# Two residual layers, one with a masked weight and one with LoRA: order of the groups and of the start changed

## The chip, the cores and the metric

The kernel runs on one core of one Trainium2 chip. The metric is the device time of one execution in microseconds (us), the median of several.

## The reference

For each of 8 batch elements, x has 256 rows and 1024 columns. D = 1024, the LoRA rank R is 16. In float32:

```
# layer 0: a weight that is changed by a mask, with its own coefficient for each batch element
y = x + x @ W0.T + b0 + coeff[b] * (x @ (2 * mask[b] - 1))
# layer 1: a fixed weight and the LoRA pair of the element's slot
A, B = lora_As[slot[b]], lora_Bs[slot[b]]
z = y + y @ W1.T + b1 + 2.0 * ((y @ A) @ B)
```

## The kernel before, in words

**Precision.** TensorE multiplies operands of the type float32r (fp32r in the rows). Each operand is split into a high part (written by ScalarE as float32r) and a low part (the difference, made by VectorE), and each product is three: high by high, high by low, low by high.

**Layer 0 of a batch element.** The weight of element b is W0 + identity + 2 coeff x mask - coeff. It is made in eight blocks k of 128 x 1024. The mask block is loaded by SP into one of four slots of `ring`. VectorE writes `sums` (weights_sum, L463) over it, ScalarE makes wc_hi from this (weights_high, L338), VectorE makes wc_lo (weights_low, L470), both in rings of four. A mask slot is free again when wc_lo of its block is done. TensorE takes 16 products with wc_hi (layer0_high, L258) and 8 with wc_lo (layer0_low, L267) for each block, summing into four PSUM banks y_ps. Then ScalarE and VectorE write y_two, the parts of y, out of them (y_high L357, y_low L493). x is split the same way (x_high L351, x_low L486).

**Layer 1.** For two halves s of 128 rows, the 16 + 1024 columns of [A, W1] are cut into three groups g, each with its own PSUM bank z_ps. A group is 24 products (layer1_group, L290): eight k by three. Group 0 holds h = y A. h is scaled, split into h_rows (h_high L363, h_low L501), transposed by TensorE (turn_h, L303) and copied to h_stack (h_copy, L368). A closing product of h_stack and b_stack (the parts of B and b1) ends each group (close_group, L311). Then ScalarE copies z_ps to z_rows (z_copy, L375), and stores each half from its own DMA queue (store).

**W1 and LoRA.** W1 is loaded once, through the same ring slots as the masks. GpSimd adds the identity to its diagonal block (L237), ScalarE writes w1_hi (w1_high, L345) and VectorE w1_lo (w1_low, L481). The LoRA pair is loaded for each element (load_lora on SP, one transfer for a_raw and four for b_raw). ScalarE writes the high parts of A and B (lora_high, L386 and L387), and GpSimd both low parts (lora_low, L218 and L221):

```
            def lora_low(b):
                pool.wait_ge(lora_hi_done, 2 * (b + 1))
                pool.tensor_tensor(w1_lo[:, :, 0:R], a_raw[:], w1_hi[:, :, 0:R].bitcast(F32),
                                   ALU.subtract).then_inc(lora_lo_done, 1)
                pool.wait_ge(lora_lo_done, 2 * b + 1)
```

The two low parts of element b bring lora_lo_done to 2b + 1 and 2b + 2. load_lora(b) on SP waits for lora_lo_done >= 2b.

**What sets the order.** Every engine runs an order written out by hand, and semaphores join them. Nothing is planned by a tool. On each engine what stands behind a waiting instruction waits too. Before, TensorE ran layer 0 and layer 1 of one element after the other. At the start SP loads W0, mask and x of element 0 in turns, GpSimd adds the identity to W0's diagonal blocks (L214), makes the parts of b1 (L226 to L231), and then the diagonals of W1. TensorE warms up with 30 transposes (L246).

## Time and profile before

| what | us |
|---|---|
| median of 3 runs | 424.15 (424.01 to 424.44) |
| the profiled execution | 426.43 |
| its span, first to last instruction | 424.6 |
| TensorE products busy | 389.6 (92%) |
| VectorE busy | 228.5 (54%) |
| ScalarE busy | 158.8 (37%) |
| GpSimd busy | 46.1 (11%) |

The span lies inside the profiled execution's time. Busy time of TensorE counts products that overlap in its pipeline, so it is not the share of its peak. PE is TensorE's products, PEld its weight loads, DVE is VectorE, ACT ScalarE, POOL GpSimd, SP the engine that only issues transfers; a q behind a name (SPq, ACTq) is that engine's instruction queue. L12 is line 12 of the kernel.

### The profile page before, as it was taken

Reading aid. Unit: us, or ns where it says so; the run is one execution under the profiler, and the core shown is the slowest. Engines: PE = TensorE matmul, PEld = TensorE weight load, DVE = VectorE, ACT = ScalarE, POOL = GpSimd, SP = SyncE. Lnnn points to the kernel's source line nnn. Section 1 sums busy time; section 2 is a strip of 40 time slices with the busy share of each in tenths; the row PEclk is TensorE's granted clock in tenths of the full one; section 3 lists DMA queues with packets and bytes.
Section 4 is the critical chain, followed back from the end, with each engine's and each line's share of the span. In section 5 each row is a group of like instructions: output and inputs, shape, how many; then the busy total and the mean of one; then the engine's idle time right before and its main releaser. Section 6 shows DMA issues by size and latency. Waiting matters only on the chain.

```text
span 424.6 us, 6715 instructions
## 1 busy us (share of the span) xinstructions
PE 389.6 (92%) x2782; PEld 385.9 (91%) x2782; DVE 228.5 (54%) x265; ACT 158.8 (37%) x282; POOL 46.1 (11%) x43
## 2 busy tenths in 40 slices
PE   5986049999999999999999999999999999999997
PEld 5986049999999999999999999999999999999996
DVE  1788747752584727752474717843475717843300
ACT  2433715341544325341444324341444324432311
POOL 1338340020002000020001100020000100020000
PEclk9799659999999999999999999999999999999999
DMA  8985780665047520665046520675036520520011
GB/s 270 398 271 182 250 277 4 229 220 175 2 145 210 194 78 2 213 234 181 0 137 220 190 82 0 203 243 181 2 129 211 206 82 2 198 100 2 0 51 49
DMA packets 21220, 61.80 MB, mean 146 GB/s; under 512 B 3012, under 2 KB 4292, under 8 KB 21190
## 3 DMA queue, kind: packets, MB, share of 16 engines
q1 hardware_dynamic: 18304, 52.96, 38.2%
q10 hardware_dynamic: 2886, 8.41, 4.9%
q8 instruction: 22, 0.36, 0.3%
q14 instruction: 8, 0.07, 0.0%
HBM read 52.97 MB, written 8.39 MB: 144 GB/s over the span
## 4 chain that ended last, share of the span: by engine, by line
PE 83%; DMA 8%; DVE 3%; issue 2%; ACT 2%; POOL 1%; SPq 1%; ACTq 0%; DVEq 0%
PE z_ps L290 44%; PE y_ps L258 25%; PE y_ps L267 11%; DMA ring<-in_mask 4%; DMA ring<-in_w 2%; PE z_ps L311 2%; DMA w_t<-in_w 2%; ACT y_two L357 1%; DVE wc_lo L470 1%; POOL ring L237 1%; DVE w_lo L481 1%; DVE y_two L493 1%; ACT w_hi L345 1%; PE t_ps L303 0%; DVE ring L463 0%
## 5 line engine op out<-in xcount | busy, mean ns | idle before, releaser
L290 PE MATMUL z_ps<-w_hi,y_two 128*128 128x344 f32 (+1 forms) x768 | 191.5, 325 | 23.2 <-DVE w_lo L481 17.4
L290 PEld LDWEIGHTS z_ps<-w_hi,y_two 128*128 128x128 f32 x768 | 136.4, 190 | 25.2 <-DVE w_lo L481 17.6
L258 PE MATMUL y_ps<-x_two,wc_hi 128*128 128x256 f32 x1024 | 135.1, 285 | 2.7 <-ACT wc_hi L338 2.7
L258 PEld LDWEIGHTS y_ps<-x_two,wc_hi 128*128 128x128 f32 x1024 | 129.5, 194 | 3.0 <-DVE x_two L486 3.0
L290 PE MATMUL z_ps<-w_lo,y_two 128*128 128x344 f32 (+1 forms) x384 | 124.3, 324 | 0.0
L470 DVE SCALAR_TENSOR_TENSOR wc_lo<-ring,coeff_neg,wc_hi 128x1024 fp32r<-128x1024 f32 x64 | 91.5, 1432 | 51.3 <-ACT wc_hi L338 51.0
L338 ACT ACTIVATE wc_hi<-ring,coeff_neg 128x1024 fp32r<-128x1024 f32 x64 | 73.6, 1151 | 69.7 <-PE y_ps L267 41.4
L463 DVE SCALAR_TENSOR_TENSOR ring<-ring,coeff_two,w_t 128x1024 f32<-128x1024 int32 x64 | 82.0, 1290 | 6.5 <-DMA ring<-in_mask 6.4
L267 PE MATMUL y_ps<-x_two,wc_lo 128*128 128x256 f32 x512 | 73.2, 286 | 4.7 <-DVE wc_lo L470 4.7
L290 PEld LDWEIGHTS z_ps<-w_lo,y_two 128*128 128x128 f32 x384 | 73.1, 190 | 0.0
L267 PEld LDWEIGHTS y_ps<-x_two,wc_lo 128*128 128x128 f32 x512 | 66.7, 194 | 5.8 <-DVE wc_lo L470 5.8
L493 DVE SCALAR_TENSOR_TENSOR y_two<-y_ps,b_cols,y_two 128x256 fp32r<-128x256 f32 x64 | 25.8, 476 | 64.7 <-ACT y_two L357 64.7
L357 ACT ACTIVATE y_two<-y_ps,b_cols 128x256 fp32r<-128x256 f32 x64 | 24.1, 486 | 67.1 <-PE y_ps L267 67.1
L218 POOL TENSOR_TENSOR w_lo<-a_raw,w_hi 128x128 fp32r<-128x128 f32 x8 | 3.7, 457 | 300.5 <-ACT b_stack L387 300.5
L375 ACT ACTIVATE z_rows<-z_ps 128x344 f32<-128x344 f32 (+1 forms) x48 | 20.0, 451 | 38.2 <-PE z_ps L311 38.2
L501 DVE SCALAR_TENSOR_TENSOR h_rows<-z_ps,h_rows 128x16 fp32r<-128x16 f32 x32 | 4.1, 170 | 45.7 <-ACT h_rows L363 45.7
L486 DVE TENSOR_TENSOR x_two<-x_raw,x_two 128x512 fp32r<-128x512 f32 x32 | 21.1, 696 | 12.3 <-ACT x_two L351 12.3
L363 ACT ACTIVATE h_rows<-z_ps 128x16 fp32r<-128x16 f32 x32 | 4.1, 181 | 54.6 <-PE z_ps L290 54.6
L351 ACT ACTIVATE x_two<-x_raw 128x512 fp32r<-128x512 f32 x32 | 18.5, 626 | 5.7 <-DMA x_raw<-in_x 5.7
L221 POOL TENSOR_TENSOR b_stack<-b_raw,b_stack 32x1024 fp32r<-32x1024 f32 x8 | 19.0, 2380 | 0.6
L481 DVE TENSOR_TENSOR w_lo<-ring,w_hi 128x1024 fp32r<-128x1024 f32 x8 | 11.2, 1436 | 4.5 <-ACT w_hi L345 4.5
L311 PE MATMUL z_ps<-b_stack,h_stack 66*128 66x344 f32 (+1 forms) x48 | 12.7, 318 | 0.0
(25 smaller groups left out, 74.0 us busy)
## 6 DMA issues: line engine op xcount, KB each, us to landing
ring<-in_mask SPq DMA_DIRECT2D x64, 512.0 KB, 3.6
x_raw<-in_x SPq DMA_DIRECT2D x32, 256.0 KB, 5.8
out<-z_rows ACTq DMA_DIRECT2D x14, 512.0 KB, 5.0
w_t<-in_w SPq DMA_DIRECT2D x8, 512.0 KB, 7.3
ring<-in_w SPq DMA_DIRECT2D x8, 512.0 KB, 4.3
b_raw<-in_lora_b SPq DMA_DIRECT2D x32, 64.0 KB, 2.6
out<-z_rows ACTq DMA_DIRECT2D x2, 340.0 KB, 2.2
a_raw<-in_lora_a SPq DMA_DIRECT2D x8, 64.0 KB, 2.8
```

Of the source, the lines that this page charges most:

```text
L221: pool.tensor_tensor(b_stack[2 * R:LR, :], b_raw[2 * R:LR, :], b_stack[2 * R:LR, :].bitcast(F32), ALU.subtract).then_inc(lora_lo_done, 1)
L258: pe.matmul(ys, w, x_two[:, k, n, :], start=(k == 0 and o % PAIR == 0 and n == 0), stop=False, skip_group_check=True)
L267: ins = pe.matmul(ys, w, x_two[:, k, 0, :], start=False, stop=(k == KT - 1), skip_group_check=True)
L290: ins = pe.matmul(z_ps[g][:, 0:EDGES[g + 1] - EDGES[g]], ys[:, k, s * P:(s + 1) * P], w[:, k, EDGES[g]:EDGES[g + 1]], start=(k == 0 and n ...
L311: pe.matmul(z_ps[g][:, lo:EDGES[g + 1] - EDGES[g]], h_stack[0:KS, s * P:(s + 1) * P], b_stack[0:KS, EDGES[g] + lo - R:EDGES[g + 1] - R], s ...
L338: act.activation(wc_hi[:, k % RING, :], sums[:, mask_entry(b, k) % RING, :], ACT.Identity, bias=coeff_neg[:, b:b + 1]).then_inc(wc_hi_done, 1)
L357: act.activation(y_two[:, b % 2, 0, o, :], y_ps[g][:, (o % PAIR) * T:(o % PAIR + 1) * T], ACT.Identity, bias=b0_cols[:, o:o + 1]).then_inc ...
L375: act.activation(z_rows[:, s, EDGES[g] + lo - R:EDGES[g + 1] - R], z_ps[g][:, lo:EDGES[g + 1] - EDGES[g]], ACT.Copy).then_inc(z_done, 1)
L463: dve.scalar_tensor_tensor(out=sums[:, e % RING, :], in0=ring[:, e % RING, :], scalar=coeff_two[:, b:b + 1], in1=w0_t[:, k, :], op0=ALU.mu ...
L470: dve.scalar_tensor_tensor(out=wc_lo[:, k % RING, :], in0=sums[:, mask_entry(b, k) % RING, :], scalar=coeff_neg[:, b:b + 1], in1=wc_hi[:, ...
L486: dve.tensor_tensor(x_two[:, PAIR * g:PAIR * (g + 1), 1, :], x_raw[:, PAIR * g:PAIR * (g + 1), :], x_two[:, PAIR * g:PAIR * (g + 1), 0, :] ...
L493: dve.scalar_tensor_tensor(out=y_two[:, b % 2, 1, o, :], in0=y_ps[g][:, (o % PAIR) * T:(o % PAIR + 1) * T], scalar=b0_cols[:, o:o + 1], in ...
```

## The change

It has three parts.

1. The last group of layer 1 (s = 1, g = 2) with its closing product moves behind layer 0 of the next element (layer1_last). ScalarE and VectorE run y_high, y_low, x_high and x_low at the head of their turn, and z_copy and store of that last group come behind them. lora_high is split: the A half stands behind z_copy(a, 1, 1), the B half behind the moved z_copy and store.
2. Element 0 is worked in half blocks of 512 columns, each with a wait of its own (parts). Layer 1 of element 0 opens with layer1_first, which goes through W1 block by block for all three groups of s = 0. Group (0, 1, 0) uses the bank y_ps[3].
3. W0's blocks 1 to 7 are loaded from ScalarE's queue, the first block in halves from SP's, and the first x through ScalarE's queue. SP loads the LoRA pair of element 0 behind the fourth W1 block.

lora_low on GpSimd is as before. The diff, cut to its core:

```diff
+        def parts(b, k, h=1):
+            return 2 * k + h + 1 if b == 0 else KT * (b + 1) + k + 1
...
+        def z_bank(b, s, g):
+            return y_ps[XG - 1] if (b, s, g) == (0, 1, 0) else z_ps[g]
...
+            sp.dma_start(w0_t[:, 0, 0:HALF], w0[0, :, 0:HALF]).then_inc(w0_first, 16)
+            sp.dma_start(ring[:, 0, 0:HALF], mask_v[0, 0][:, 0:HALF]).then_inc(mask_first, 16)
+            sp.dma_start(w0_t[:, 0, HALF:D], w0[0, :, HALF:D]).then_inc(w0_in[0], 16)
+            sp.dma_start(ring[:, 0, HALF:D], mask_v[0, 0][:, HALF:D]).then_inc(ring_in[0], 16)
+            for k in range(1, KT):
                 load_mask(0, k)
-                if k % PAIR == 0:
-                    load_x(0, k // PAIR)
+                if k % PAIR == 1 and k < KT - 1:
+                    load_x(0, k // PAIR + 1)
+            for k in range(RING):
+                load_w1(k)
             sp.wait_ge(ids_in, 16)
             load_lora(0)
-            for k in range(KT):
+            for k in range(RING, KT):
...
             def layer0_high(b, k):
                 pe.wait_ge(x_lo_done, XG * b + k // PAIR + 1)
-                pe.wait_ge(wc_hi_done, KT * b + k + 1)
+                if b > 0:
+                    pe.wait_ge(wc_hi_done, parts(b, k))
                 for o in range(KT):
+                    if b == 0 and o % HT == 0:
+                        pe.wait_ge(wc_hi_done, parts(b, k, o // HT))
                     if k == 0 and o % PAIR == 0:
                         need(pe, y_lo_done, KT * (b - 1) + o + PAIR)
+                    if b == 1 and k == 0 and o == KT - PAIR:
+                        pe.wait_ge(z_done, NG + 1)
...
+            def products(b, s, g, k):
+                y_hi, y_lo = y_two[:, b % 2, 0], y_two[:, b % 2, 1]
+                for n, (ys, w) in enumerate(((y_hi, w1_hi), (y_hi, w1_lo), (y_lo, w1_hi))):
+                    ins = pe.matmul(z_bank(b, s, g)[:, 0:EDGES[g + 1] - EDGES[g]], ys[:, k, s * P:(s + 1) * P],
+                                    w[:, k, EDGES[g]:EDGES[g + 1]],
+                                    start=(k == 0 and n == 0), stop=(g == 0 and k == KT - 1 and n == 2),
+                                    skip_group_check=True)
+                if g == 0 and k == KT - 1:
+                    ins.then_inc(h_full, 1)
+            def layer1_first():
+                pe.wait_ge(lora_lo_done, 1)
+                for k in range(KT):
+                    pe.wait_ge(w1_lo_done, k + 1)
+                    pe.wait_ge(y_lo_done, k + 1)
+                    for g in range(NG):
+                        products(0, 0, g, k)
             def layer1_group(b, s, g, ks=range(KT)):
                 if ks[0] == 0:
-                    need(pe, z_done, NG * (ST * b + s - 1) + g + 1)
-                    if b == 0 and s == 0 and g == 0:
-                        pe.wait_ge(w1_lo_done, KT)
+                    if (b, s, g) != (0, 1, 0):
+                        need(pe, z_done, NG * (ST * b + s - 1) + g + 1)
                     if s == 0 and g == 0:
-                        pe.wait_ge(lora_lo_done, 2 * (b + 1))
-                y_hi, y_lo = y_two[:, b % 2, 0], y_two[:, b % 2, 1]
+                        pe.wait_ge(lora_lo_done, 2 * b + 1)
                 for k in ks:
                     if s == 0 and g == 0:
                         pe.wait_ge(y_lo_done, KT * b + k + 1)
-                    for n, (ys, w) in enumerate(((y_hi, w1_hi), (y_hi, w1_lo), (y_lo, w1_hi))):
-                        ins = pe.matmul(z_ps[g][:, 0:EDGES[g + 1] - EDGES[g]], ys[:, k, s * P:(s + 1) * P],
-                                        w[:, k, EDGES[g]:EDGES[g + 1]],
-                                        start=(k == 0 and n == 0), stop=(g == 0 and k == KT - 1 and n == 2),
-                                        skip_group_check=True)
-                if g == 0 and ks[-1] == KT - 1:
-                    ins.then_inc(h_full, 1)
+                    products(b, s, g, k)
...
                     pe.wait_ge(h_stacked, ST * b + s + 1)
-                pe.matmul(z_ps[g][:, lo:EDGES[g + 1] - EDGES[g]], h_stack[0:KS, s * P:(s + 1) * P],
+                    pe.wait_ge(lora_lo_done, 2 * (b + 1))
+                pe.matmul(z_bank(b, s, g)[:, lo:EDGES[g + 1] - EDGES[g]], h_stack[0:KS, s * P:(s + 1) * P],
...
             def layer1(b):
                 for s in range(ST):
-                    layer1_group(b, s, 0)
-                    layer1_group(b, s, 1, range(KT // 2))
-                    turn_h(b, s)
-                    layer1_group(b, s, 1, range(KT // 2, KT))
-                    close_group(b, s, 0)
-                    close_group(b, s, 1)
-                    layer1_group(b, s, 2)
-                    close_group(b, s, 2)
+                    if b > 0:
+                        layer1_group(b, s, 0)
+                        layer1_group(b, s, 1, range(HT))
+                        turn_h(b, s)
+                        layer1_group(b, s, 1, range(HT, KT))
+                        close_group(b, s, 0)
+                        close_group(b, s, 1)
+                    elif s == 0:
+                        layer1_first()
+                        layer1_group(0, 1, 0, range(HT))
+                        turn_h(0, 0)
+                        layer1_group(0, 1, 0, range(HT, KT))
+                        close_group(0, 0, 0)
+                        close_group(0, 0, 1)
+                    if s == 0 and b > 0:
+                        layer1_group(b, 0, 2)
+                    if s == 0:
+                        close_group(b, 0, 2)
+                    if s == 1 and b == 0:
+                        layer1_group(0, 1, 1, range(HT))
+                        turn_h(0, 1)
+                        layer1_group(0, 1, 1, range(HT, KT))
+                        close_group(0, 1, 0)
+                        close_group(0, 1, 1)
+            def layer1_last(b):
+                layer1_group(b, 1, 2)
+                close_group(b, 1, 2)
             pe.wait_ge(ident_done, 1)
             warm_up(30)
-            for b in range(NB):
+            layer0(0)
+            layer1(0)
+            for b in range(1, NB):
                 layer0(b)
+                layer1_last(b - 1)
                 layer1(b)
+            layer1_last(NB - 1)
...
-            def lora_high(b):
+            def lora_a_high(b):
                 act.wait_ge(lora_in, 16 * 5 * (b + 1))
+                if b > 0:
+                    act.wait_ge(z_full, NG * (ST * b - 1) + 1)
+                act.activation(w1_hi[:, :, 0:R], a_raw[:], ACT.Copy).then_inc(lora_hi_done, 1)
+            def lora_b_high(b):
                 need(act, z_full, NG * ST * b)
-                act.activation(w1_hi[:, :, 0:R], a_raw[:], ACT.Copy).then_inc(lora_hi_done, 1)
                 act.activation(b_stack[0:LR, :], b_raw[0:LR, :], ACT.Copy).then_inc(lora_hi_done, 1)
...
+            for k in range(1, KT):
+                act.dma_start(w0_t[:, k, :], w0[k]).then_inc(w0_in[k], 16)
...
-            for k in range(RING):
-                w1_high(k)
-            lora_high(0)
+            w1_high(0)
+            w1_high(1)
+            lora_a_high(0)
             act.wait_ge(b0_in, 16)
             for g in range(XG):
                 y_high(0, g)
-            for k in range(RING, KT):
+            for k in range(2, KT):
                 w1_high(k)
-            for b in range(1, NB):
+            lora_b_high(0)
+            for b in range(1, NB + 1):
                 a = b - 1
+                if a > 0:
+                    for g in range(XG):
+                        y_high(a, g)
+                if b < NB:
+                    for g in range(XG):
+                        x_high(b, g)
+                if a > 0:
+                    z_copy(a - 1, 1, 2)
+                    store(a - 1, 1)
+                    lora_b_high(a)
                 h_high(a, 0)
-                x_high(b, 0)
-                x_high(b, 1)
                 h_copy(a, 0)
-                x_high(b, 2)
-                x_high(b, 3)
-                weights_high(b, 0)
+                if b < NB:
+                    weights_high(b, 0)
                 z_copy(a, 0, 0)
                 z_copy(a, 0, 1)
-                weights_high(b, 1)
+                if b < NB:
+                    weights_high(b, 1)
+                    weights_high(b, 2)
                 z_copy(a, 0, 2)
                 store(a, 0)
                 h_high(a, 1)
-                weights_high(b, 2)
+                if b < NB:
+                    weights_high(b, 3)
                 h_copy(a, 1)
-                weights_high(b, 3)
                 z_copy(a, 1, 0)
                 z_copy(a, 1, 1)
-                z_copy(a, 1, 2)
-                store(a, 1)
-                lora_high(b)
-                for k in range(RING, KT):
-                    weights_high(b, k)
-                for g in range(XG):
-                    y_high(b, g)
-            a = NB - 1
+                if b < NB:
+                    lora_a_high(b)
+                    for k in range(RING, KT):
+                        weights_high(b, k)
+            store(NB - 1, 1, 0, 2)
+            z_copy(NB - 1, 1, 2)
+            store(NB - 1, 1, 2, 3)
...
-            x_low(0, 0)
-            for k in range(KT - 1):
-                step(0, k)
-                if k % PAIR == 0 and k < KT - PAIR:
-                    x_low(0, k // PAIR + 1)
-            weights_low(0, KT - 1)
-            for k in range(RING):
-                w1_low(k)
+            for k in range(KT):
+                weights_sum(0, k, 0)
+                if k % PAIR == 0:
+                    x_low(0, k // PAIR)
+                weights_sum(0, k, 1)
+                weights_low(0, k, 0)
+                weights_low(0, k, 1)
+            w1_low(0)
+            w1_low(1)
             dve.wait_ge(b0_in, 16)
             for g in range(XG):
                 y_low(0, g)
-            for k in range(RING, KT):
+            for k in range(2, KT):
                 w1_low(k)
             for b in range(1, NB):
                 a = b - 1
+                if a > 0:
+                    for g in range(XG):
+                        y_low(a, g)
+                for g in range(XG):
+                    x_low(b, g)
                 h_low(a, 0)
-                x_low(b, 0)
-                x_low(b, 1)
-                x_low(b, 2)
-                x_low(b, 3)
                 weights_sum(b, 0)
                 step(b, 0)
                 step(b, 1)
+                step(b, 2)
                 h_low(a, 1)
-                for k in range(2, KT):
+                for k in range(3, KT):
                     step(b, k)
-                for g in range(XG):
-                    y_low(b, g)
+            for g in range(XG):
+                y_low(NB - 1, g)
```

## Rows read from the trace of the kernel before

**Rows 1.** The page, its first line.

```profile
span 424.6 us, 6715 instructions
...
```

**Rows 2.** Chain of waits: start us, us, what (x instructions merged).

```profile
...
59.13 8.09 PE z_ps L290 x36
...
85.45 1.91 PE y_ps L258 x16
...
105.60 1.92 PE y_ps L258 x16
...
109.30 5.96 PE z_ps L290 x36
...
121.49 5.75 PE z_ps L290 x36
...
129.55 3.77 PE z_ps L290 x24
133.48 1.91 PE y_ps L258 x16
...
```

**Rows 3.** Waits: engine line <- releaser: total us, times, longest us.

```profile
...
PE z_ps L290 <- DVE y_two L493: 5.8, 7, 0.8
...
PE y_ps L267 <- DVE wc_lo L470: 4.7, 4, 2.2
...
```

**Rows 4.** Timeline of ScalarE, 104 to 137 us: start, us, operation.

```profile
...
107.79 3.02 ACT L357 ACTIVATE y_two<-y_ps,b_cols 128x256 fp32r<-128x256 f32 x8 [9.59 <-PE y_ps L267]
...
113.55 1.15 ACT L351 ACTIVATE x_two<-x_raw 128x512 fp32r<-128x512 f32 x2
...
133.52 0.46 ACT L375 ACTIVATE z_rows<-z_ps 128x344 f32<-128x344 f32 x1 [3.29 <-PE z_ps L311]
...
134.45 0.31 ACT L386 ACTIVATE w_hi<-a_raw 128x128 fp32r<-128x128 f32 x1 [0.47 <-ACT z_rows L375]
134.66 1.04 ACT L387 ACTIVATE b_stack<-b_raw 64x1024 fp32r<-64x1024 f32 x1
...
```

**Rows 5.** Timeline of GpSimd, 104 to 137 us.

```profile
...
135.79 0.46 POOL L218 TENSOR_TENSOR w_lo<-a_raw,w_hi 128x128 fp32r<-128x128 f32 x1 [45.07 <-ACT b_stack L387]
...
```

**Rows 6.** Timeline of VectorE, 104 to 137 us.

```profile
...
108.67 3.23 DVE L493 SCALAR_TENSOR_TENSOR y_two<-y_ps,b_cols,y_two 128x256 fp32r<-128x256 f32 x8 [9.14 <-ACT y_two L357]
...
116.23 1.29 DVE L486 TENSOR_TENSOR x_two<-x_raw,x_two 128x512 fp32r<-128x512 f32 x2 [0.72 <-ACT x_two L351]
...
```

**Rows 7.** Timeline of all engines, 0 to 90 us.

```profile
...
12.23 1.28 DVE L470 SCALAR_TENSOR_TENSOR wc_lo<-ring,coeff_neg,wc_hi 128x1024 fp32r<-128x1024 f32 x1
...
24.81 0.33 SPq L158 DMA_DIRECT2D ring<-in_mask  x1
...
26.59 1.89 SPq L178 DMA_DIRECT2D b_raw<-in_lora_b  x4
...
34.19 5.37 DVE L470 SCALAR_TENSOR_TENSOR wc_lo<-ring,coeff_neg,wc_hi 128x1024 fp32r<-128x1024 f32 x2
...
52.57 2.59 POOL L237 TENSOR_TENSOR ring<-ring,ident 128x128 f32<-128x128 f32 x1 [2.52 <-DMA ring<-in_w]
...
```

**Rows 8.** The page, transfers: KB each, median us from issue to landing.

```profile
...
ring<-in_w SPq DMA_DIRECT2D x8, 512.0 KB, 4.3
b_raw<-in_lora_b SPq DMA_DIRECT2D x32, 64.0 KB, 2.6
...
```

**Rows 9.** Windows: us, busy by engine, granted clock (PEclk), DMA share, GB/s.

```profile
...
7.10:9.10 2.00, 0.00 (x0) 0.00 (x0) 0.45 (x1) 1.11 (x2) 0.00 (x0) 1.00 1.00 401
9.30:15.80 6.50, 5.98 (x26) 5.72 (x27) 3.38 (x5) 2.14 (x3) 2.10 (x3) 0.50 1.03 413
16.00:46.60 30.60, 21.02 (x167) 20.00 (x165) 25.32 (x19) 12.41 (x14) 16.09 (x13) 1.00 0.76 252
46.80:63.60 16.80, 4.47 (x15) 4.48 (x16) 10.07 (x13) 7.37 (x13) 6.25 (x5) 0.50 0.81 277
63.80:424.60 360.80, 352.18 (x2546) 350.01 (x2544) 187.36 (x228) 133.84 (x250) 19.90 (x14) 1.00 0.37 123
...
```

More of the change, by code:

```diff
@@ L30, in cond_residual_two_layers @@
     KS = LR + 2
+    HALF = D // 2
+    HT = KT // 2
     assert PAIR == 2 and ST == 2 and XG == 4 and LR == 64 and KT == 2 * RING and NB > 2
@@ L211, in _ @@
             for k in range(KT):
-                pool.wait_ge(w0_in[k], 16)
+                pool.wait_ge(w0_first if k == 0 else w0_in[k], 16)
                 blk = w0_t[:, k, k * P:(k + 1) * P]
@@ L335, in weights_high @@
             def weights_high(b, k):
-                act.wait_ge(sum_done, KT * b + k + 1)
                 block_read(act, b, k - RING)
-                act.activation(wc_hi[:, k % RING, :], sums[:, mask_entry(b, k) % RING, :], ACT.Identity,
-                               bias=coeff_neg[:, b:b + 1]).then_inc(wc_hi_done, 1)
+                e = mask_entry(b, k)
+                for lo, hi in ((0, HALF), (HALF, D)) if b == 0 else ((0, D),):
+                    act.wait_ge(sum_done, parts(b, k, lo // HALF) if b == 0 else parts(b, k))
+                    act.activation(wc_hi[:, k % RING, lo:hi], sums[:, e % RING, lo:hi], ACT.Identity,
+                                   bias=coeff_neg[:, b:b + 1]).then_inc(wc_hi_done, 1)
             def w1_high(k):
@@ L375, in z_copy @@
                 act.activation(z_rows[:, s, EDGES[g] + lo - R:EDGES[g + 1] - R],
-                               z_ps[g][:, lo:EDGES[g + 1] - EDGES[g]], ACT.Copy).then_inc(z_done, 1)
+                               z_bank(b, s, g)[:, lo:EDGES[g + 1] - EDGES[g]], ACT.Copy).then_inc(z_done, 1)
             def store(b, s, g0=0, g1=NG):
@@ L442, in _ @@
-            a = NB - 1
-            for s in range(ST):
-                h_high(a, s)
-                h_copy(a, s)
-                z_copy(a, s, 0)
-                z_copy(a, s, 1)
-                store(a, s, 0, 2)
-                z_copy(a, s, 2)
-                store(a, s, 2, 3)
-            for s in range(ST):
-                act.wait_ge(z_out[s], 16 * (NB + 1))
+                if b < NB:
+                    lora_a_high(b)
+                    for k in range(RING, KT):
+                        weights_high(b, k)
@@ L456, in _, with weights_sum @@
+            store(NB - 1, 1, 0, 2)
+            z_copy(NB - 1, 1, 2)
+            store(NB - 1, 1, 2, 3)
+            for s in range(ST):
+                act.wait_ge(z_out[s], 16 * (NB + s))
         @block.vector
         def _(dve):
-            def weights_sum(b, k):
+            def weights_sum(b, k, h=None):
                 e = mask_entry(b, k)
-                ring_filled(dve, e)
-                if b == 0:
+                lo, hi = (0, D) if h is None else (HALF * h, HALF * (h + 1))
+                if (b, k, h) == (0, 0, 0):
+                    dve.wait_ge(mask_first, 16)
+                else:
+                    ring_filled(dve, e)
+                if b == 0 and k // HT == h:
@@ L462, in weights_sum @@
                     dve.wait_ge(w0_diag, k + 1)
-                dve.scalar_tensor_tensor(out=sums[:, e % RING, :], in0=ring[:, e % RING, :],
-                                         scalar=coeff_two[:, b:b + 1], in1=w0_t[:, k, :],
+                elif b == 0:
+                    dve.wait_ge(w0_in[k], 16)
+                dve.scalar_tensor_tensor(out=sums[:, e % RING, lo:hi], in0=ring[:, e % RING, lo:hi],
+                                         scalar=coeff_two[:, b:b + 1], in1=w0_t[:, k, lo:hi],
@@ L465, in weights_sum, with weights_low @@
                                          op0=ALU.mult, op1=ALU.add).then_inc(sum_done, 1)
-            def weights_low(b, k):
-                dve.wait_ge(wc_hi_done, KT * b + k + 1)
-                dve.wait_ge(sum_done, KT * b + k + 1)
-                dve.scalar_tensor_tensor(out=wc_lo[:, k % RING, :], in0=sums[:, mask_entry(b, k) % RING, :],
-                                         scalar=coeff_neg[:, b:b + 1], in1=wc_hi[:, k % RING, :].bitcast(F32),
+            def weights_low(b, k, h=None):
+                lo, hi = (0, D) if h is None else (HALF * h, HALF * (h + 1))
+                n = parts(b, k) if h is None else parts(b, k, h)
+                dve.wait_ge(wc_hi_done, n)
+                dve.wait_ge(sum_done, n)
+                dve.scalar_tensor_tensor(out=wc_lo[:, k % RING, lo:hi], in0=sums[:, mask_entry(b, k) % RING, lo:hi],
+                                         scalar=coeff_neg[:, b:b + 1], in1=wc_hi[:, k % RING, lo:hi].bitcast(F32),
```

21 lines of the change are left out of this document (11 added, 10 removed).

## The prediction

> **What bounds the kernel now.** I read the page first: TensorE is busy for most of the 424.6 us span [rows 1]. The chain of waits then shows where it is not. From 85.45 us on it repeats every 48.03 us (85.45 to 133.48) [rows 2]: layer 0 ends at 105.60 + 1.92 + 0.96 = 108.48, layer 1 begins at 109.30, and the next layer 0 at 133.48. The list of waits puts seven waits of 0.8 us on the residual y_two (L493) [rows 3]. So the steady part holds 0.82 us of idle TensorE in each batch, and a first stretch of 36 products that takes 5.96 instead of 5.75 us, as it follows y_two block by block: 1.03 us a batch, 7.2 us in all. That is all that the steady part has to give. The other reserve is the start: layer 1 of batch 0 begins only at 59.13 [rows 2].
>
> **The steady part: what is removed, and what comes in its place.** Behind layer 0 of batch b now stand the 24 products and the closing product of batch b-1's last group: 133.48 - 129.55 = 3.93 us [rows 2]. In that time ScalarE and VectorE can make y_two, so the 1.03 us go. But look at what layer 1 of b waits for besides y_two. layer1_group(b, 0, 0) waits for lora_lo_done >= 2b + 1, the low part of the A columns, which GpSimd makes in lora_low (L216). That function is not in the diff, and its first line waits for lora_hi_done >= 2(b + 1), both high copies. The change splits these: A's is early, but B's (lora_b_high) now stands on ScalarE behind y_high(a), x_high(b) and z_copy(a-1, 1, 2) of the same turn. So A's low part, which needs nothing of B, comes after B's copy. Before, both copies were made early in layer 0 (134.45 and 134.66 [rows 4]) and nobody waited.
>
> I walk that queue on the clock of batch 1, where layer 0 ends at 108.48. The eight y_high run from 107.79 for 3.02 us, to 110.81. Four x_high follow, 1.15 us for each two [rows 4]: 2.30, to 113.11. The moved group is over at 108.48 + 3.93 = 112.41, so z_copy can start at 113.11. From z_copy's start to that of B's copy it is 134.66 - 133.52 = 1.14 us, store's issue included, less 0.21 for A's copy, which is no longer between them: 0.93 [rows 4]. From B's copy to GpSimd's subtraction it is 135.79 - 134.66 = 1.13, the subtraction takes 0.46 [rows 5], and waking TensorE 0.14 (the first y_low ends 0.49 after 108.67, TensorE starts at 109.30 [rows 2, 6]). Sum 2.66: layer 1 starts at 115.77, TensorE has been idle for 3.36 us. VectorE's four x_low end near 114.5 (108.67 + 3.23 + 4 x 0.65 [rows 6]), so GpSimd meets nobody. In the last batch there is no x_high, z_copy starts right at 112.45, and the idle time is 2.70. Together 6 x 3.36 + 2.70 = 22.9 us.
>
> Other queues: load_lora(b) on SP now waits until that subtraction, with masks 4 to 7 of b behind it. Their ring slots are freed by wc_lo(b, 0) some 9 us into layer 1, later than that; cost nothing, and if the cover were gone, layer 0 would start late by as much. The sums of batch b start after h_low(a, 0), sooner in layer 1 than now; layer 0 has four blocks ready. The wait for z_done = 4 before y_ps[3] (once, batch 1) has 12 products in front of it, 1.4 us, against two z copies: nothing.
>
> From layer 0 of batch 1 to the end: 424.6 - 85.45 = 339.15 before; plus 3.93 for batch 0's group, which was before that point; less 7.2; plus 22.9: 358.8 us.
>
> **Layer 1 of batch 0.** Before it took 85.45 - 59.13 = 26.32 us, some 2.3 of it by the half clock [rows 2]. Without the moved group 22.4. Two waits are new. Group (0, 1, 1) needs z_ps[1], free only after two copies: 0.6 us. And the transpose of h(0, 1) waits for h_low(0, 1), which on VectorE stands behind step(1, 2). With T for the moment when h(0, 0) is full: sums 0 and 1 until T + 3.1, wc_lo 0 waits for wc_hi 0 (behind h_copy) and ends at T + 5.9, wc_lo 1 waits for wc_hi 1 (behind two z copies) and ends at T + 8.4, sum 3 and wc_lo 2 until T + 10.9, h_low until T + 11.1. TensorE reaches the transpose at T + 7.9. It waits 3.2 us. Sum 22.4 + 3.8 = 26.2.
>
> **The start.** "Layer 1 follows W1" does not happen, for the reason above: layer1_first waits for lora_lo_done >= 1, so for lora_b_high(0), which ScalarE makes after w1_high(7), and GpSimd after its eight w1 diagonals. All of W1 is there when it starts. When is that? Halves save one half of sum, copy and difference on the first block, 1.6 us: wc_lo 0 ends at 11.9 instead of 12.23 + 1.28 = 13.5 [rows 7]; TensorE's first product stays about where it is, as ScalarE now issues eight more transfers before its first copy. Then VectorE is the bound: four half operations of 0.65 [rows 6] and 0.15 of waiting for ScalarE make 2.75 a block, 7 x 2.75 + 3 x 0.65 for x_low = 21.2, to 33.1. GpSimd's b1 chain falls into this: beside it two full operations took 5.37 us instead of 2.5 and ended at 39.56 [rows 7]. I add 3.5 for it and 0.9 for the diagonals: wc_lo 7 ends at 37.5 (36 to 39).
> From there, in us behind it: SP issues the fourth W1 block, and only then the lora transfers; 1.78 from the block's issue to the first of b_raw, 1.4 to the last [rows 7]; landing 2.6 by its median, 3.1 taken [rows 8]: 6.4. lora_a_high waits for that and has y_high behind it: 6.8. y_high and y_low 108.67 + 3.23 - 107.79 = 4.1 [rows 4, 6]: 10.9. w1_low 2 and 3, 1.2 each: 13.3; W1's last block is issued then and lands 4.3 later [rows 8]: 17.7. Diagonal 0.5, or 2.59 beside VectorE [rows 7], 1.5 taken; w1_high, as wide as B's copy, 1.05; B's copy 1.14; subtraction and waking 0.7: 22.1. So layer 1 starts at 37.5 + 22.1 = 59.6 (57.5 to 62), against 59.13: what the halves give, the late lora load takes back. W0 on ScalarE's queue changes no sum: from 9.30 to 15.80 the engines of both queues were full, share 1.03 at 413 GB/s [rows 9]. The Trainium skill (Trainium Kernel Development and Optimization, Key Constraints) says that several issuing engines save issue time only; by it the term is the same nothing, and the trace agrees as far as it goes, one queue filled the engines.
>
> Sum without the clock: 59.6 + 26.2 + 358.8 = 444.6 us, 20.0 above the span.
>
> **The clock.** Eight idle times of 2.7 to 3.4 us are new in a stream that ran at full clock. The granted clock was 1.00 in the idle time from 7.10 to 9.10, and 0.50 (1.2 GHz) from 9.30 to 15.80; it was 1.00 (2.4 GHz) from 16.00 to 46.60, with a wait of 2.2 us in it [rows 3, 9]. So an idle time near 2 us has been answered in both ways, and these are longer. I take six falls of eight. Price of one: TensorE worked from 59.13 to 63.80 at half clock, 4.67 us, half of it lost: 2.3 (8.09 for 36 products instead of 5.75 says the same [rows 2]). The lower bound is nothing, the upper 5.98 / 2 = 3.0 [rows 9]. 6 x 2.3 = 13.8.
>
> Span 444.6 + 13.8 = 458.4, +33.8. The profiled execution took 426.43 with 424.6 of span; the median is 424.15. Forecast 424.15 + 33.8 = 458.0.
>
> **Rivals.** (A) The forecast: the queue behind B's copy stalls layer 1 in each batch, and the clock falls at four to eight of the stalls: 451 to 468. Chance 0.68. (B) The same stalls, but the clock mostly holds (none to three falls): 442 to 451. For it speaks the 2.2 us wait without a fall, against it 7.10 to 9.30. Chance 0.28. The Trainium skill (TensorE: Matmul & The Clock Gate, What's actually happening) says that the ramp penalty is under 1% of a typical kernel; by that rule the clock would add at most some 4 us, so about 448, in B. Its section on HAM oscillation describes the contrary, a pause in each turn that makes each turn start cold. (C) The other side: the chain to A's low part fits under the moved group, and the time is 424.15 + 0.5 - 0.1 + 3.9 - 7.2 = 421, or 416 if layer 1 of batch 0 starts 5 us sooner as well. It decides where the eight waits sum to less than 2.9 us, 0.4 for each of the seven batches and nothing in batch 0. The walk gives 3.36, with 2.66 of it behind z_copy, which can't start before 112.41. Chance 0.03, with no change 0.01.
>
> The measurement of this kernel tells about 0.2% from no change. Faster 0.03, same 0.01, slower 0.96. The low end of the range, 443, is B with one early start; the high end, 466, is A with eight falls and 62 for the start cut at one in ten.
>
> **What would show it.** Waits: TensorE L290's successor waits on GpSimd's L218 successor, seven times near 3.3 us (the last 2.7), and no longer on y_two. The period is 50.4 us plus the clock. The granted clock is below 1.00 behind several stalls. GpSimd's A subtraction follows B's copy at once. At the start TensorE's layer 1 begins at 57.5 to 62, in one block of 72 products without waits for W1. wc_lo 7 ends at 36 to 39. One wait of 3.2 us for h_low in batch 0. I am wrong if GpSimd's subtraction comes before layer 0 ends, or if the waits are there and something else has shrunk.

## The result, and the profile after

| | us |
|---|---|
| median after (4 runs) | 457.77 (457.31 to 458.28) |
| median before beside it (4 runs) | 424.29 (424.01 to 425.89) |
| ratio after to before | 1.078 (95% interval 1.075 to 1.081) |
| forecast | 458.0, range 443 to 466 |
| span after, granted clock over it | 456.5, 0.94 |

The change makes the kernel 7.8% slower. The waits of TensorE after the change, out of the list of waits (engine, line, what it waited for, total us, times, longest):

```profile
PE z_ps L304 <- issue: 20.1, 7, 2.9
PE z_ps L304 <- POOL w_lo L232: 18.3, 1, 18.3
...
PE t_ps L338 <- issue: 2.8, 1, 2.8
...
PE z_ps L304 <- ACT z_rows L439: 0.6, 1, 0.6
```

The seven waits of 0.8 us for y_two [rows 3] are gone, and seven waits of up to 2.9 us, 20.1 in all, stand in their place. The list calls their end "issue": it found no releaser for them. The queues of the other engines tell who it is. Here are ScalarE and GpSimd in the turn that answers to [rows 4, 5] (timelines, start and us):

```profile
109.47 3.03 ACT L421 ACTIVATE y_two<-y_ps,b_cols 128x256 fp32r<-128x256 f32 x8 [9.65 <-PE y_ps L290]
112.33 2.23 ACT L415 ACTIVATE x_two<-x_raw 128x512 fp32r<-128x512 f32 x4
114.41 0.50 ACT L439 ACTIVATE z_rows<-z_ps 128x344 f32<-128x344 f32 x1
...
115.34 1.06 ACT L456 ACTIVATE b_stack<-b_raw 64x1024 fp32r<-64x1024 f32 x1 [0.43 <-ACT z_rows L439]
```

```profile
116.47 0.45 POOL L232 TENSOR_TENSOR w_lo<-a_raw,w_hi 128x128 fp32r<-128x128 f32 x1 [53.09 <-ACT b_stack L456]
117.00 2.35 POOL L235 TENSOR_TENSOR b_stack<-b_raw,b_stack 32x1024 fp32r<-32x1024 f32 x1
```

GpSimd had been idle for 53.09 us, waiting for B's high part. It ends A's low part at 116.92, and TensorE starts at 117.02. The moved group was over at 113.77 + 0.32 = 114.09 (timeline of TensorE):

```profile
113.77 0.32 PE L347 MATMUL z_ps<-b_stack,h_stack 66*128 66x344 f32 x1
117.02 0.56 PE L304 MATMUL z_ps<-w_hi,y_two 128*128 128x352 f32 x1 [2.93 <-issue]
```

And the clock (windows of TensorE: us, busy, granted clock, DMA share, GB/s), in the wait and in the 5.1 us behind it:

```profile
114.02:117.02 3.00, 0.07 (x1) 1.00 0.41 171
117.02:118.72 1.70, 1.70 (x6) 0.52 0.06 17
118.72:120.42 1.70, 1.70 (x8) 0.50 0.00 0
120.42:122.12 1.70, 1.70 (x12) 0.97 0.38 121
```

It is 1.00 through the wait, and 0.52 and 0.50 (1.2 GHz) once work is back, from 117.02 to 120.42. The chain of waits gives the price of each fall by the first 36 products behind a wait; these are three turns, the first of them also with its undisturbed second half (5.76, against 5.75 in [rows 2]):

```profile
87.11 1.92 PE y_ps L278 x16
...
117.02 7.52 PE z_ps L304 x36
...
130.78 5.76 PE z_ps L304 x36
...
138.84 1.92 PE y_ps L278 x16
...
168.75 7.34 PE z_ps L304 x36
...
220.28 8.71 PE z_ps L304 x36
```

The seven took 7.52, 7.34, 8.71, 7.50, 7.52, 7.48 and 7.40 us: 13.2 us over 7 x 5.76. The first turn is 138.84 - 87.11 = 51.73 us long, against 48.03; less its 1.76 us of slow products it is 49.97, where the forecast had 50.4.

The start: 72 products without a wait for W1 between them, from 60.59, and layer 0 of batch 1 at 87.11 (59.13 and 85.45 before, [rows 2]).

```profile
60.59 14.06 PE z_ps L304 x72
```

### The profile page after: what moved, and what is told of

It is laid out like the page before. It is cut to its first block, busy times and chain, and to the rows that moved or that the text cites. A ratio compares the mean times of both kernels' runs of the same rounds, so it can differ in the third digit from the quotient of the medians.

```text
span 456.5 us, 6779 instructions
## 1 busy us (share of the span) xinstructions
PE 402.7 (88%) x2782; PEld 397.4 (87%) x2782; DVE 225.9 (49%) x281; ACT 161.4 (35%) x290; POOL 39.1 (9%) x43
## 4 chain that ended last, share of the span: by engine, by line
PE 74%; ACT 10%; issue 7%; DVE 4%; DMA 2%; ACTq 2%; SPq 1%; POOL 0%; DVEq 0%
PE z_ps L304 37%; PE y_ps L278 24%; PE y_ps L290 11%; ACT y_two L421 4%; ACT x_two L415 3%; DVE ring L542 2%; ACT wc_hi L402 2%; PE z_ps L347 1%; DMA ring<-in_w 1%; ACTq L465 1%; PE y_ps L304 1%; ACT z_rows L439 1%; DVE wc_lo L551 1%; DVE y_two L574 1%; DMA b_raw<-in_lora_b 1%
## 5 line engine op out<-in xcount | busy, mean ns | idle before, releaser
L304 PE MATMUL z_ps<-w_hi,y_two 128*128 128x344 f32 (+1 forms) x752 | 197.1, 339 | 39.0 <-issue 20.1
L304 PEld LDWEIGHTS z_ps<-w_hi,y_two 128*128 128x128 f32 x752 | 141.9, 202 | 41.8 <-issue 21.9
L278 PE MATMUL y_ps<-x_two,wc_hi 128*128 128x256 f32 x1024 | 136.8, 287 | 6.0 <-DVE x_two L567 4.2
L304 PE MATMUL z_ps<-w_lo,y_two 128*128 128x344 f32 (+1 forms) x376 | 126.9, 338 | 0.0
L551 DVE SCALAR_TENSOR_TENSOR wc_lo<-ring,coeff_neg,wc_hi 128x1024 fp32r<-128x1024 f32 (+1 forms) x72 | 86.8, 1210 | 49.9 <-ACT wc_hi L402 48.5
L402 ACT ACTIVATE wc_hi<-ring,coeff_neg 128x1024 fp32r<-128x1024 f32 (+1 forms) x72 | 75.8, 1056 | 67.6 <-PE y_ps L290 50.5
L542 DVE SCALAR_TENSOR_TENSOR ring<-ring,coeff_two,w_t 128x1024 f32<-128x1024 int32 (+1 forms) x72 | 84.6, 1187 | 6.4 <-DMA ring<-in_mask 6.4
L304 PEld LDWEIGHTS z_ps<-w_lo,y_two 128*128 128x128 f32 x376 | 76.1, 202 | 0.0
L439 ACT ACTIVATE z_rows<-z_ps 128x344 f32<-128x344 f32 (+1 forms) x47 | 20.0, 459 | 33.8 <-PE z_ps L347 33.8
L567 DVE TENSOR_TENSOR x_two<-x_raw,x_two 128x512 fp32r<-128x512 f32 x32 | 22.3, 752 | 2.1 <-ACT x_two L415 2.1
L432 ACT ACTIVATE h_stack<-t_ps 66x128 fp32r<-66x128 f32 x16 | 4.4, 273 | 21.2 <-PE t_ps L338 21.2
```

Of the source, the lines that this page charges most:

```text
L278: pe.matmul(ys, w, x_two[:, k, n, :], start=(k == 0 and o % PAIR == 0 and n == 0), stop=False, skip_group_check=True)
L304: ins = pe.matmul(z_bank(b, s, g)[:, 0:EDGES[g + 1] - EDGES[g]], ys[:, k, s * P:(s + 1) * P], w[:, k, EDGES[g]:EDGES[g + 1]], start=(k == ...
L402: act.activation(wc_hi[:, k % RING, lo:hi], sums[:, e % RING, lo:hi], ACT.Identity, bias=coeff_neg[:, b:b + 1]).then_inc(wc_hi_done, 1)
L439: act.activation(z_rows[:, s, EDGES[g] + lo - R:EDGES[g + 1] - R], z_bank(b, s, g)[:, lo:EDGES[g + 1] - EDGES[g]], ACT.Copy).then_inc(z_do ...
L542: dve.scalar_tensor_tensor(out=sums[:, e % RING, lo:hi], in0=ring[:, e % RING, lo:hi], scalar=coeff_two[:, b:b + 1], in1=w0_t[:, k, lo:hi] ...
L551: dve.scalar_tensor_tensor(out=wc_lo[:, k % RING, lo:hi], in0=sums[:, mask_entry(b, k) % RING, lo:hi], scalar=coeff_neg[:, b:b + 1], in1=w ...
```

## The experiments

Kernel n is the kernel of experiment n; where nothing else is said, its edit is made to the changed kernel. The edits are shortened, and x_high(b, 0..3) stands for four calls. Each kernel was timed beside the kernel before on the same chip. Before measured 425.1 to 425.3 us there, 0.8 to 1.0 more than beside the changed kernel, so differences against the changed kernel are uncertain by 1 us.

**1. A's low part waits for A's high part alone, from batch 1 on.**

```diff
 def lora_low(b):
-    pool.wait_ge(lora_hi_done, 2 * (b + 1))
+    pool.wait_ge(lora_hi_done, 2 * b + 1 if b > 0 else 2)
     pool.tensor_tensor(w1_lo[:, :, 0:R], a_raw[:], w1_hi ...)
+    pool.wait_ge(lora_hi_done, 2 * (b + 1))
     pool.wait_ge(lora_lo_done, 2 * b + 1)
```

> The changed kernel with one thing more: from element 1 on, GpSimd's low part of the A columns waits for ScalarE's high part of A alone, and only the low part of B waits for B's. My theory (layer 1 waits for A's low part, which is late only because it stands behind B's high part, and the clock falls in that wait): the seven waits of 20.1 us in all go, and the 13.2 us of half clock behind them go with them, so 457.8 - 33.3 = 424.5 us, granted clock 1.00 from batch 1 on. Rival one (the place of the wait is taken by the next in the queue, y_two or h behind the four x_high): a wait of 1 to 2 us stays in each batch and some of the falls, 435 to 445 us. Rival two (the slower first products have another cause than the wait, for instance VectorE reading the same banks): the waits go, the slow products stay, 437.7 us.

Measured 426.26 us, ratio 1.002 (1.000 to 1.004). The span fell from 456.5 to 423.8. The seven waits and their slow products are gone; layer 1 follows the moved group without a gap (chain of waits, where line 305 is the changed kernel's 304):

```profile
110.77 3.79 PE z_ps L305 x24
...
114.72 5.75 PE z_ps L305 x36
```

One line of waiting cost 31.5 us. The time is 1.8 us above the expected 424.5. The kernel before stood 1.0 us higher beside this kernel than beside the changed one, and the 2.8 us wait in batch 0 brought a fall of the clock here, which it did not in the changed kernel's profile: the 12 products behind it took 2.94 instead of 1.88 us (chain of waits):

```profile
84.01 2.94 PE z_ps L305 x12
```

What is left is a change that gains in the steady part and loses as much at the start; kernel 4 tells the two apart.

**2. The wait is filled with products.**

```diff
 layer1_last(b - 1)
+for _ in range(17):
+    pe.matmul(t_ps[:, 0:344], y_two[:, (b - 1) % 2, 0, 0, P:2 * P], w1_hi[:, 0, EDGES[2]:EDGES[3]], start=True, stop=True)
 layer1(b)
```

> The changed kernel, with 17 more products of 344 columns on TensorE between the moved group and layer 1 of each batch from 1 on; they write a bank that nobody reads then (0.157 us each, 2.67 us of the 2.9 us wait), so no term of the output changes. Layer 1 still waits for A's low part as long as before. My theory of the clock (it falls because TensorE is idle, and the slow first products are nothing else): the waits stay at 2.9 us, filled, the clock stays 1.00, and the 13.2 us go: 457.8 - 13.2 = 444.6 us. Rival (the first products are slow for another reason): no change, 457.8 us. Rival (17 products are too many): up to 2 us more.

Measured 446.82, ratio 1.051 (1.048 to 1.054). The clock stays at 1.00 and the first 36 products take 6.00 us (chain of waits):

```profile
115.11 2.65 PE t_ps L386 x17
...
118.06 6.00 PE z_ps L304 x36
```

So 11 of the 33.5 us are the clock alone: the wait is as long, only not idle. The time is 2.2 us above the expected. The seven first stretches took 5.96 to 6.00 and not 5.76 us, 1.5 us in all; and the 2.8 us wait in batch 0 brought a fall as in kernel 1, with the same 2.94 us for the 12 products behind it.

**3. The same early low part for batch 0 too**, behind the fourth W1 diagonal.

```diff
     pool.tensor_tensor(blk, blk, ident[:], ALU.add).then_inc(w1_diag, 1)
+    if k == RING - 1:
+        lora_a_low(0)
+lora_b_low(0)
-for b in range(NB):
-    lora_low(b)
+for b in range(1, NB):
+    lora_a_low(b)
+    lora_b_low(b)
```

> As the first of these kernels, but for batch 0 too: GpSimd makes the low part of A's columns of batch 0 behind the fourth diagonal of W1, so layer 1 of batch 0 can really go through W1 block by block. My theory: its first products start near 47 us instead of 60.6, and by the time that the last W1 block is split (60.2 us) only its own nine products are left, so h(0, 0) is full near 61.7 instead of 73.7. Then h_low(0, 0) stands behind four x_low until 65, and layer 0 of batch 1 starts some 14 us behind that, near 79 to 80 instead of 87.1: 424.5 - 7.5 = 417 us. Rival (TensorE's products are so slow at half clock, 2.8 us a block, that they stay behind W1): 420 to 422. Rival (W1 arrives later, as GpSimd waits for the LoRA load between two diagonals): 420 to 424.

Measured 416.01, ratio 0.979 (0.976 to 0.982). Now layer 1 does follow W1 (timeline of TensorE): its first product is at 47.20, and the last W1 block lets it wait once.

```profile
47.20 0.63 PE L311 MATMUL z_ps<-w_hi,y_two 128*128 128x352 f32 x1 [5.54 <-DVE y_two L581]
...
60.57 0.43 PE L311 MATMUL z_ps<-w_hi,y_two 128*128 128x352 f32 x1 [1.26 <-DVE w_lo L569]
```

**4. The steady part alone**, on the start of before, with the early low part. The orders of ScalarE and VectorE in the turn are those of the change.

```diff
 # kernel before, and:
 for b in range(1, NB):
     layer0(b)
+    layer1_last(b - 1)
     layer1(b)      # without its last group
```

> The kernel before with only the first part of the change, the last group of layer 1 behind the next layer 0, and A's low part waiting for A's high part alone; the start is that of before. My theory: seven waits for y_two of 0.8 us and the 0.2 us in the first products behind each go, and nothing else: 424.3 - 7.2 = 417.1 us. Rival (the order of the queues in the turn, x_high and x_low ahead of h, costs TensorE waits elsewhere in the batch): 418 to 424. If this comes out at 417 and the first of these kernels at 424.5, the start as changed costs about 7 us by itself.

Measured 418.97, ratio 0.985 (0.983 to 0.988), 6.3 us under its own before. That is 1.9 us above the expected 417.1 and in the range of the rival, but the rival's cause is not there: from layer 0 of batch 1 (81.14) to the end the list of TensorE's waits is empty, and a turn takes 128.18 - 81.14 = 47.04 us, 1.0 less than before, as expected. 1.0 us of the miss is the kernel before, which measured that much more beside this kernel than beside the changed one; the rest stays open. Against kernel 1, whose turn is as long, it is the start alone: 426.26 - 418.97 = 7.3 us. The start of the change, as long as nothing follows W1, is a loss: a start of layer 1 that comes later (58.16 here, 60.50 in kernel 1) and the two waits in batch 0.

**5. The LoRA pair of batch 0 ahead of W1**, on kernel 3.

```diff
-for k in range(RING):
-    load_w1(k)
 sp.wait_ge(ids_in, 16)
 load_lora(0)
-for k in range(RING, KT):
+for k in range(KT):
     load_w1(k)
```

> The third kernel (A's low part early in all batches) with one thing undone: SP loads the LoRA pair of batch 0 before the first four W1 blocks, as in the kernel before, instead of behind them. My theory (the late LoRA load holds ScalarE before y_high for 4.6 to 5 us, and y_low, w1_low 2 and 3 and W1's last two blocks follow in its train): the last W1 block is split near 56.5 instead of 60.5, and the time is 416.0 - 3.6 = 412.4 us. Rival (W1's last block is late because of its own ring slots and not of that load): 416.

Measured 412.31, ratio 0.968 (0.965 to 0.971), 3.7 us under kernel 3. y_low starts at 42.47 instead of 46.57 and the last w1_low at 55.46 instead of 59.29 (timeline of VectorE, kernel 5):

```profile
42.47 3.21 DVE L581 SCALAR_TENSOR_TENSOR y_two<-y_ps,b_cols,y_two 128x256 fp32r<-128x256 f32 x8
...
55.46 1.23 DVE L569 TENSOR_TENSOR w_lo<-ring,w_hi 128x1024 fp32r<-128x1024 f32 x1 [1.50 <-ACT w_hi L416]
```

**6. Whole blocks in batch 0**: the start of before, but layer1_first and kernel 3's early low part.

```diff
-for lo, hi in ((0, HALF), (HALF, D)) if b == 0 else ((0, D),):
+for lo, hi in ((0, D),):
...
-w1_low(0)
-w1_low(1)
+for k in range(RING):
+    w1_low(k)
 dve.wait_ge(b0_in, 16)
```

> The start of the kernel before (whole blocks, W0 on SP's queue, LoRA before W1, w1_low 0 to 3 before y_low), but layer 1 of batch 0 goes through W1 block by block, and A's low part is early; the steady part is the changed one. My theory (half blocks bring nothing, as wc_lo 7 ended at 39.81 with them and at 39.56 without): the same as the kernel with the LoRA load first, 412.4 us, within 1.5. Rival (the halves do bring something that the LoRA load hides): 414.5 to 416.

Measured 411.92, ratio 0.968 (0.966 to 0.971), the time of kernel 5. But two things differ from kernel 5: the halves are gone, and W0 is back on SP's queue, which is worth 1.9 us in kernel 8. So the equal times do not show that the halves bring nothing. wc_lo 7 ended at 35.18 + 3.45 = 38.63 here, at 39.76 in kernel 5 (halves, W0 on ScalarE's queue), and at 37.46 in kernel 8 (halves, W0 on SP's).

**7. h first**, on kernel 6, in batch 1's turn. ScalarE's order follows: h_high(0, 1) stands behind the first two z copies.

```diff
 # VectorE, a == 0
+h_low(0, 0)
 x_low(1, 0..3)
-h_low(0, 0)
 weights_sum(1, 0)
+h_low(0, 1)
 step(1, 0); step(1, 1); step(1, 2)
-h_low(0, 1)
```

> The whole-block start that follows W1, and in batch 1's turn VectorE takes h_low(0, 0) before the four x_low and h_low(0, 1) behind the first sum, and ScalarE h_high(0, 1) behind the two first z copies. My theory (in batch 0 TensorE waits 3.3 us for the transpose of h(0, 0) and 1.3 for that of h(0, 1) only because these stand behind other work): about 4 us less than the same kernel without it, 408.4 us. Rival (the sums of batch 1 come later and layer 0 of batch 1 waits for them instead): 411 to 412.5.

Measured 408.37, ratio 0.961 (0.958 to 0.964), 3.55 us under kernel 6. Kernel 6 had one wait of 2.8 us for a transpose of h in TensorE's list of waits; kernel 7 has none.

**8. W0 on SP's queue**, on kernel 3.

```diff
 # SP
 for k in range(1, KT):
+    sp.dma_start(w0_t[:, k, :], w0[k])
     load_mask(0, k)
 # ScalarE
-for k in range(1, KT):
-    act.dma_start(w0_t[:, k, :], w0[k])
```

> The third kernel with W0's blocks 1 to 7 on SP's queue again, each before its mask block; x of the first group stays on ScalarE's queue. The forecast said that moving W0 changes no sum. My theory: ScalarE loads its table 4.4 us sooner, but x lands no sooner, so the first block gains about 1 us, and VectorE's own work sets the rest: 415.0 to 416.0 us against 416.0. Rival (W0 in turns with the masks lets both arrive late, masks 6 and 7 above all): 417 to 420.

Measured 414.06, ratio 0.974 (0.970 to 0.977): 1.9 us less than kernel 3. The two were timed at different times, so this is a small difference. The traces bear it out: VectorE takes up the second half of the first block at 8.41 here and at 10.32 in kernel 3, and wc_lo 7 ends at 35.91 + 1.55 = 37.46 instead of 38.01 + 1.42 = 39.43. Both expectations are missed, on the side of more gain. The changed kernel's ScalarE (its timeline) shows why: seven issues of 0.6 us, then the table, and only then its first copy, at 9.24. In kernel 8 the first copy starts at 7.14.

```profile
3.24 4.44 ACTq L465 DMA_DIRECT2D w_t<-in_w  x7
7.71 1.28 ACT L467 ACT_TABLE_LOAD   x1 [7.71 <-issue]
...
9.24 0.63 ACT L415 ACTIVATE x_two<-x_raw 128x512 fp32r<-128x512 f32 x1
```

**9. b1's parts behind the sixth W1 diagonal**, on kernel 7.

```diff
-pool.wait_ge(b1_in, 32)
-pool.tensor_copy(b_stack[LR:KS, :], b_raw[LR:KS, :])
-pool.tensor_tensor(b_stack[LR:KS, :], b_raw[LR:KS, :], b_stack[LR:KS, :], ALU.subtract)
-pool.tensor_copy(b_stack[LR:LR + 1, :], b_raw[LR:LR + 1, :])
...
     if k == RING - 1:
         lora_a_low(0)
+    if k == RING + 1:
+        pool.wait_ge(w1_diag, k + 1)
+        pool.wait_ge(b1_in, 32)
+        pool.tensor_copy(b_stack[LR:KS, :], b_raw[LR:KS, :])
+        pool.tensor_tensor(b_stack[LR:KS, :], b_raw[LR:KS, :], b_stack[LR:KS, :], ALU.subtract)
+        pool.tensor_copy(b_stack[LR:LR + 1, :], b_raw[LR:LR + 1, :])
```

> The whole-block kernel with h first, and GpSimd makes the three parts of b1 behind W1's sixth diagonal instead of between W0's last and W1's first. My theory (these three instructions hold up VectorE's sums and differences of blocks 6 and 7 of batch 0 by some 3.5 us, and everything up to layer 1 of batch 0 follows in their train): 408.4 - 3.0 = 405.4 us. Rival (the chain now holds up w1_low or the last W1 diagonals as much): 408 to 409.

Measured 404.38, ratio 0.952 (0.949 to 0.955), the fastest of all. wc_lo 7 ends at 31.35 + 2.68 = 34.03 us; in kernel 7 it ended at 34.54 + 3.45 = 37.99, 4.0 us later, as much as the time differs.

**10. x_high behind B's high part**, on the changed kernel.

```diff
-x_high(b, 0..3)
 z_copy(a - 1, 1, 2)
 store(a - 1, 1)
 lora_b_high(a)
+x_high(b, 0..3)
```

> The changed kernel with the four x_high of each turn behind lora_b_high instead of ahead of z_copy; A's low part still waits for B's high part. The forecast's walk says that the chain can't start before z_full of the moved group, whatever stands before it, and takes 2.66 us from there. So the wait falls from 2.9 to 2.6 us in six batches, the clock still falls: 457.8 - 2 = 455.8 us. Rival (the length of ScalarE's queue is what makes the wait, so 2.1 us less in each): 440 to 445.

Measured 455.67, ratio 1.072 (1.068 to 1.076). The waits are 18.2 us in all, 2.6 the longest: ScalarE's queue is shorter by four copies and only 0.3 us a turn comes of it. z_copy's place behind the moved group sets the wait.

```profile
PE z_ps L304 <- issue: 18.2, 7, 2.6
```

**11. The moved group alone, as in the change**: kernel 4 with lora_low as it was.

```diff
-pool.wait_ge(lora_hi_done, 2 * b + 1)
+pool.wait_ge(lora_hi_done, 2 * (b + 1))
...
-pool.wait_ge(lora_hi_done, 2 * (b + 1))
```

> The kernel before with the first part of the change alone, exactly as in the change: the last group behind the next layer 0, lora_high split, lora_low as it was. The start is that of before. My theory (the whole loss is in this part, and the other two parts cost some 7 us more): the 419.0 us of the same kernel with an early low part of A, plus 20.1 us of waits and 13.2 us of half clock: 452 us. Rival (the loss needs the new start too): below 440.

Measured 452.81, ratio 1.066 (1.063 to 1.069). That is 33.8 us over kernel 4. The seven waits are 20.2 us, as in the changed kernel:

```profile
PE z_ps L290 <- issue: 20.2, 7, 3.0
```

**12. All of it with half blocks.**

```diff
+def lora_a_low(b):
+    pool.wait_ge(lora_hi_done, 2 * b + 1)
...
+    sp.dma_start(w0_t[:, k, :], w0[k])
...
+load_lora(0)
 for k in range(RING):
     load_w1(k)
...
+h_low(0, 0)
...
+    if k == RING + 1:
+        pool.wait_ge(w1_diag, k + 1)
```

It is the changed kernel with the edits of 3, 5, 7, 8 and 9.

> The changed kernel's half blocks with all that was found put together: A's low part early, W0 on SP's queue, LoRA before W1, h first in batch 1's turn, b1 behind W1's sixth diagonal. If the terms add up (412.3 for the kernel with the LoRA load first, less 2.0 for W0, less 3.6 for h, less 3.0 for b1): 403.7 us, and the halves are worth about 1.7 us against the same with whole blocks. Rival (they cover each other, as the end of the W1 stream binds): 405 to 408.

Measured 405.67, ratio 0.955 (0.951 to 0.958). The terms don't add up, the rival holds: wc_lo 7 ends at 34.37, 0.3 us after that of kernel 9 (34.03), and the last two w1_low start at 52.02 against 51.30. This start is 1.3 us slower than that of kernel 9 instead of 1.7 faster. It has more in it than the halves, though: w1_high and w1_low of W1's blocks 2 and 3 stand behind y_high and y_low here and ahead of them in kernel 9, and y_low starts at 37.56 against 41.85. VectorE waited 2.62 us for w1_high ahead of the last two w1_low, 1.51 in kernel 9. Which of the two costs the time no run tells apart, so what half blocks are worth by themselves stays open.

## Why the prediction was right

| term | forecast | measured |
|---|---|---|
| layer 1 of batch 0 starts | 59.6 (57.5 to 62) | 60.59 |
| from there to layer 0 of batch 1 | 26.2 | 26.52 |
| seven waits | 22.9 | 20.1 |
| the clock | 13.8 | 13.2 |
| span | 458.4 | 456.5 |

That the median came out 0.2 us from the forecast is partly luck. The span was 1.9 us too high. The forecast put the growth of the span on before's median, but before's profiled execution, from which the growth is reckoned, was 2.3 us above that median (426.43 against 424.15), and the changed kernel's only 0.5 above its own (458.28 against 457.77). The two errors nearly cancel.

**The main step** held: lora_low's first wait ties A's low part to B's high part, and that stands behind z_copy of the moved group. Kernel 1 changes this wait alone and takes 31.5 us off; kernel 11 has it without the new start and pays 33.8 us against kernel 4. Kernel 10 confirms the floor: the chain can't start before the moved group ends, and the forecast's 2.66 us from there was 2.6.

**The wait** was 2.93 us and not 3.36. Nearly all of the difference lies in "four x_high follow, 1.15 us for each two": ScalarE started the first at 112.33, ahead of y_high's end, and z_copy at 114.41, 2.08 later instead of 2.30. In the last turn, without x_high, it was 2.60 for 2.70. The 0.93 and 1.13 us of the chain behind were met to the hundredth (115.34 - 114.41, 116.47 - 115.34).

**The clock.** Forecast were six falls at 2.3 us. There were seven, one at each wait in front of layer 1, at 1.6 to 3.0 us, 1.9 on average; the eighth wait, 2.8 us in batch 0, was followed by none in this profile, and by one in kernels 1, 2 and 10, with the same 2.82 us. Number and price were off in opposite directions, so that 13.2 for 13.8 is in part luck as well. Rival (B), none to three falls, is out, and so is a price under 1% of the span: 13.2 of 456.5 us are 2.9%. Kernel 2 shows that idleness brings the falls: with the same wait filled, none of the seven is left. The Trainium skill (TensorE: Matmul & The Clock Gate, HAM oscillation) describes a pause in each turn that makes each turn start cold; here a pause of 2.9 us in a turn of 51.7 does it.

**The start** came out 1.0 us late, as the sum of two errors. wc_lo 7 ended at 39.81, past the stated 36 to 39. One term that failed is "four half operations of 0.65": that is the length of x_low, and sums and differences of half blocks took 0.70 to 0.82 us. Three half sums took 0.95, each beside a diagonal of GpSimd (at 17.01, 23.97 and 32.93). So a block took 3.0 to 3.3 us, 3.7 with x_low, and not 2.75 and 3.4. The b1 chain was rightly sized, 3.5 forecast and some 3.3 measured. The other is the first block, which ended at 12.8 and not 11.9: ScalarE's seven issues of W0 took 4.44 us, its first copy started at 9.24 instead of 7.99, and "TensorE's first product stays about where it is" was wrong too (10.65 against 9.80).

```profile
38.39 1.42 DVE L551 SCALAR_TENSOR_TENSOR wc_lo<-ring,coeff_neg,wc_hi 128x512 fp32r<-128x512 f32 x2 [0.19 <-ACT wc_hi L402]
```

Against that the train behind wc_lo 7 was shorter, 20.8 us for 22.1. And "W0 on ScalarE's queue changes no sum" was wrong: kernel 8 puts about 2 us on it. It was argued from the DMA engines, which were full either way, and put nothing for ScalarE itself, which is late by its issues. The lora load's part, "what the halves give, the late lora load takes back", was right in its second half (kernel 5, 3.7 us). Of its first half only this is shown: the first block ended 0.7 us sooner than before (12.81 against 13.51), not 1.6, and with W0 on ScalarE's queue nothing of it was left at wc_lo 7 (39.81 against 39.56). What the halves give without that queue stays open (kernels 6, 8 and 12).

**"Layer 1 follows W1" doesn't happen** in the changed kernel, as forecast, and the cause is the same wait: kernel 3 mends it and gains 10.3 us over kernel 1.

**Batch 0** had its two waits, 0.6 us for z_ps[1] and 2.8 for the transpose of h(0, 1) where 3.2 were forecast. Kernel 7 removes the wait for h against kernel 6 by order alone.

## What to carry to other kernels

When a helper waits once for two products of another engine, splitting the producer moves the consumer's early half to the later of the two: look for every wait on the semaphore that the split touches. Work that is moved under a latency covers only what isn't queued behind that work: here z_copy of the moved group stood ahead of what layer 1 needed. And a short wait repeated in each turn can cost TensorE the wait and then the clock; here that was 2.9 and another 1.9 us.
